# Sixteen-head attentions: scores as one pass over rounded parts and rests, made a second time with the keys on the partitions

## The reference

```
x = x + tanh(g_xattn[0]) * L0_xattn(layernorm(x), ctx, mask, ...)     # stage 0: 16 heads of 8 features, key mask
x = x + tanh(g_ffn[0])   * L0_ffn(layernorm(x), ...)                  # stage 1: 16 experts, 4 taken, and a shared one
x = x + tanh(g_xattn[1]) * L1_xattn(...)                              # stage 2: one head, gated
x = x + tanh(g_ffn[1])   * L1_ffn(...)                                # stage 3: 8-bit fake-quantised weights, LoRA
x = x + tanh(g_xattn[2]) * L2_xattn(...)                              # stage 4: 8 heads of 64
x = x + tanh(g_ffn[2])   * L2_ffn(...)                                # stage 5: 8 experts, 2 taken, and a shared one
x = x + tanh(g_xattn[3]) * L3_xattn(layernorm(x), ctx, ctx, ...)      # stage 6: 16 heads of 8 features, no mask
x = x + tanh(g_ffn[3])   * L3_ffn(layernorm(x), ...)                  # stage 7: 64 experts, 6 taken, and a shared one
```

```
q = heads(x_n @ Wq + bq); k = heads(ctx @ Wk + bk); v = heads(ctx @ Wv + bv)
s = (q . k) / sqrt(8); s = -inf where the key is masked (stage 0)
out = (softmax(s) . v, heads side by side) @ Wo + bo
```

## Time and profile before

| | |
|---|---|
| median of 3 runs | 595.21 us |
| lowest and highest | 591.88 and 597.31 us |
| span of the profiled execution | 594.0 us, 10687 instructions |
| PE, DVE, ACT, POOL busy | 566.0, 381.8, 384.2, 243.2 us |
| the stage-0 attention, from its first scores to the last update of x | 28.1 to 91.1 us |
| the stage-6 attention, the same | 375.6 to 437.6 us |

### The profile page before, as it was taken

How to read it: one execution, slowest core, us unless ns; L and a number is a source line. 1 busy time by engine, 2 the same in 40 slices (tenths; PEclk the granted TensorE clock), 3 DMA queues, 4 the chain that set the end, 5 groups by cost and what they waited for, 6 DMA issues and landing times.

```text
span 594.0 us, 10687 instructions
## 1 busy us (share of the span) xinstructions
PE 566.0 (95%) x3685; PEld 410.5 (69%) x3689; DVE 381.8 (64%) x736; ACT 384.2 (65%) x781; POOL 243.2 (41%) x229
## 2 busy tenths in 40 slices
PE   8999998999999997999799999999999999999997
PEld 6567766787664775777555556577668788888885
DVE  1678865756741647777454666478838666666665
ACT  4277776755666447888675656677875566666663
POOL 5006673485014100111015681000024788888884
PEclk8999998999989999999989999999999999999999
DMA  8300001161000000000000102000001666666650
GB/s 253 144 2 2 2 1 33 20 168 47 7 2 1 0 1 1 1 2 1 2 0 1 40 14 67 1 2 1 2 5 42 163 171 174 184 173 180 183 132 35
DMA packets 14850, 33.54 MB, mean 56 GB/s; under 512 B 2912, under 2 KB 8432, under 8 KB 14672
## 3 DMA queue, kind: packets, MB, share of 16 engines
q1 hardware_dynamic: 14800, 32.89, 19.5%
HBM read 32.03 MB, written 0.85 MB: 55 GB/s over the span
## 4 chain that ended last, share of the span: by engine, by line
PE 76%; DVE 8%; ACT 7%; issue 6%; POOL 2%; DMA 1%; ACTq 0%; DVEq 0%; SPq 0%; POOLq 0%
PE bank L845 9%; PE bank L847 9%; PE bank L846 9%; PE bank L728 5%; PE bank L739 5%; PE bank L754 3%; PE bank L687 3%; ACT wa L1418 2%; PE bank L702 2%; PE bank L650 2%; PE bank L644 2%; PE bank L1253 2%; PE bank L1128 2%; PE bank L1142 2%; PE bank L1117 1%
## 5 line engine op out<-in xcount | busy, mean ns | idle before, releaser
L504 POOL TENSOR_TENSOR h_lo<-wc,h_hi 128x512 fp32r<-128x512 f32 x54 | 70.0, 1300 | 13.7 <-ACT h_hi L1487 13.7
L845 PE MATMUL bank<-xn_hi,w_hi 128*128 128x512 f32 x168 | 66.0, 393 | 3.4 <-DVE xn_lo L1975 3.1
L847 PE MATMUL bank<-xn_hi,w_lo 128*128 128x512 f32 x168 | 65.4, 390 | 0.0
L846 PE MATMUL bank<-xn_lo,w_hi 128*128 128x512 f32 x168 | 65.4, 389 | 0.0
L1964 DVE TENSOR_TENSOR wb<-arena,bank 128x512 f32<-128x512 f32 x64 | 44.0, 687 | 33.0 <-PE bank L847 33.0
L1487 ACT ACTIVATE h_hi<-wc 128x512 fp32r<-128x512 f32 x54 | 34.0, 633 | 37.6 <-DVE wc L1972 27.9
L496 POOL TENSOR_TENSOR w_lo<-ring,w_hi 128x384 fp32r<-128x384 f32 x42 | 42.7, 1019 | 19.1 <-ACT w_hi L1464 19.1
L1746 DVE TENSOR_TENSOR wa<-bank,row_max 128x512 f32<-128x512 f32 x64 | 44.3, 691 | 7.5 <-ACT wb L1364 4.3
L1364 ACT ACTIVATE wb<-wa 128x512 f32<-128x512 f32 x64 | 40.1, 630 | 13.7 <-DVE wa L1746 13.3
L1742 DVE TENSOR_REDUCE row_max<-bank 128x4 f32<-128x512 f32 x64 | 43.6, 682 | 5.9 <-PE bank L728 5.4
L1370 ACT ACTIVATE wc<-bank 128x512 f32<-128x512 f32 x64 | 38.0, 593 | 8.4 <-PE bank L739 7.8
(11 more groups left out here) (351 smaller groups left out, 1392.2 us busy)
## 6 DMA issues: line engine op xcount, KB each, us to landing
arena<-comb_rows SPq DMA_DIRECT2D x64, 256.0 KB, 4.1
ring<-in_experts SPq DMA_DIRECT2D x42, 192.0 KB, 2.5
ring<-in_experts SPq DMA_DIRECT2D x8, 256.0 KB, 4.0
mats<-in_mats SPq DMA_DIRECT2D x1, 1472.0 KB, 10.5
mats<-in_mats SPq DMA_DIRECT2D x1, 832.0 KB, 6.7
mats<-in_mats SPq DMA_DIRECT2D x2, 320.0 KB, 8.2
x<-in_x_t SPq DMA_DIRECT2D x1, 512.0 KB, 4.7
context<-in_ctx_t SPq DMA_DIRECT2D x1, 512.0 KB, 5.0
```

Source lines behind the costliest of these rows:

```text
L504: nc.gpsimd.tensor_tensor(h_lo[:, v % 3, :], hidden_of(v), h_hi[:, v % 3, :].bitcast(f32), ALU.subtract).then_inc(m_h_lo, 1)
L845: mm(out, w, x_, start=start, stop=False)
L846: mm(out, w, x_rest, start=False, stop=False)
L847: return mm(out, w_rest, x_, start=False, stop=stop)
```

## The change

Each group of 32 partitions now carries a head three times (24 partitions), then a mask row (24) and four rows for maxima (25 to 28). After the eviction DVE rounds one of the three copies away: keys become rounded part, rest, rounded part; queries rounded part, rounded part, rest. The product of such rows is the sum of three products, and the operands are of the rounded type f32r, which the other split products of this kernel use. So a head's scores are one f32r matmul of 32 x 128 by 32 x 128.

They are made twice. The first time queries are on the partitions, only for the maxima: DVE takes the largest over keys of two banks (1024 columns) at once, PE turns the 16 columns of maxima (`turn_tops`), and DVE adds them into the maxima rows of `q_rows`, whose partners in `k_rows` are -1 (`take_tops`). The second time keys are on the partitions (`turned_scores`) and the maxima are already subtracted; ACT takes the exponential straight from two PSUM banks, and `probs_v` uses it as it is. The subtraction, the transposes and the copies out of them are gone.

In stage 0 the mask goes into the key rows by a further matmul, ACT evicts all key rows, and the clearing and the largest-weight steps go beside the batches (`beside0`). In stage 6 `k_rows_split(1, n)` stands in stage 5: 0 and 1 ahead of norm 5, 2 and 3 behind it, 4 to 7 between `pick` and `shared(0)`; the query pieces of the first half stand ahead of the attention, those of the second in batches 0 and 1. The diff, cut to its core:

```diff
@@ gpsimd: spread_columns, now 4 copies for a matrix
-                    nc.gpsimd.tensor_copy(dst[:, :, g, :, 0:HD], wide[:, :, g, :, :]).then_inc(w_spread, 1)
+                    for e in range(2):
+                        thrice = dst[:, :, g, e, 0:3 * HD].rearrange("p m (c d) -> p m c d", c=3)
+                        nc.gpsimd.tensor_copy(thrice, wide[:, :, g, e, :].unsqueeze(2).to_broadcast([P, 4, 3, HD]))\
+                            .then_inc(w_spread, 1)
@@ tensor: k_rows_of
+                if inst == 0:
+                    ins = mm(to[:, :], mask_at[:, :], mask_neg[:, c * HALF:c * HALF + HALF], start=False, stop=True)
@@ tensor: attn
+                def by_pair(out_bank, left, right, b, p):
+                    for m_ in range(QUADS):
+                        for r in (2 * p, 2 * p + 1):
+                            rows = slice(32 * r, 32 * r + 32)
+                            last = mm(bank[out_bank + r % 2][:, m_ * P:m_ * P + P],
+                                      left[rows, m_, b * P:b * P + P], right[rows, m_, b * P:b * P + P],
+                                      start=True, stop=True)
+                    return last
                 def scores(b, p):
+                    if tb + b + p > 0:
+                        pe.wait_ge(a_max, 2 * (tb + b) + p)
+                    by_pair(0, q_rows, k_rows, b, p).then_inc(a_s, 1)
+                def turn_tops(b):
+                    pe.wait_ge(a_max, 2 * (tb + b) + 2)
+                    if b > 0:
+                        pe.wait_ge(a_exp, 2 * (tb + b) - 1)
+                    nc.tensor.transpose(bank[2][:, 0:P], top_wide[:, :], ident[:, :]).then_inc(a_top, 1)
+                def turned_scores(b, p):
+                    pe.wait_ge(a_taken, tb + b + 1)
...
+                    by_pair(2 + 2 * p, k_rows, q_rows, b, p).then_inc(a_st, 1)
...
                 scores(0, 0)
+                q_rows_of(inst, 1, range(0, 2))
                 scores(0, 1)
+                q_rows_of(inst, 1, range(2, 4))
                 for b in range(B):
+                    turn_tops(b)
+                    if b + 1 < B:
+                        scores(b + 1, 0)
+                    if b >= 2:
+                        turn_back(b - 2)
+                    if b >= 1:
+                        probs_v(b - 1, 1)
+                    if b >= 2:
+                        through_o(b - 2)
+                    turned_scores(b, 0)
+                    if b + 1 < B:
+                        scores(b + 1, 1)
+                    turned_scores(b, 1)
+                    if b >= 1:
+                        turn_o(b - 1)
+                    probs_v(b, 0)
@@ scalar: attn
+                    fn(probs[p][:, :, :], banks[:, 2 + 2 * p:4 + 2 * p, :], ACT.Exp, scale=SCALE_A).then_inc(a_exp, 1)
@@ vector
+            def rows_split(dst, raw, rounded, rests, done):
+                link(v.tensor_scalar(rounded.bitcast(f32r), raw, rest_cols[:, rests - 1:rests], None, ALU.mult))
+                v.tensor_tensor(dst, raw, rounded, ALU.subtract).then_inc(done, 1)
...
+                largest(0, 0)
+                largest(0, 1)
+                for b in range(B):
+                    take_tops(b)
+                    if b + 1 < B:
+                        largest(b + 1, 0)
+                        if b < 2:
+                            q_rows_split(inst, 4 + 2 * b)
+                        largest(b + 1, 1)
+                        if b < 2:
+                            q_rows_split(inst, 5 + 2 * b)
+                    beside(b)
+                    if b >= 1:
                         divide(b - 1)
@@ vector: stage 0
+            k_rows_split(0, 0)
             norm_rest(0)
+            for n in range(1, 4):
+                k_rows_split(0, n)
...
+            for n in range(4):
+                q_rows_split(0, n)
             for n in range(4, 8):
+                k_rows_split(0, n)
+            def beside0(b):
+                if b in (0, 1):
+                    v.tensor_reduce(w_max[:, b:b + 1], ffn_weights(b), X, ALU.max, apply_absolute_value=True)\
+                        .then_inc(d_rowmax, 1)
+                if b == 2:
+                    dve.wait_ge(d_max, 1)
+                    link(v.tensor_scalar(w_scale, w_max[:, 2:4], 1.0 / 127.0, None, ALU.mult))
+                    link(v.reciprocal(w_inv, w_scale))
+                    v.tensor_scalar(w_neg, w_scale, -1.0, None, ALU.mult).then_inc(d_scaled, 1)
+                if b == 3:
+                    v.memset(comb_pieces[:, :, :], 0.0)
+            attn(0, beside0)
@@ vector: stage 5
+            for n in range(2):
+                k_rows_split(1, n)
             norm(NORM_OF[5][0])
+            for n in range(2, 4):
+                k_rows_split(1, n)
...
             pick()
+            for n in range(4, 8):
+                k_rows_split(1, n)
@@ vector: stage 6
             norm(NORM_OF[6][0])
-            attn(1)
+            for n in range(4):
+                q_rows_split(1, n)
+            attn(1, lambda b: None)
```

More of the change, by code:

```diff
@@ L721, in scores, with probs_v @@
                         pe.wait_ge(a_q_rows, 8 * inst + 8)
-                    if b > 0:
[L723 to L747, removed]
+                    if tb + b + p > 0:
[3 more added lines that the diff above has]
+                    pe.wait_ge(a_max, 2 * (tb + b) + 2)
+                    if b > 0:
+                        pe.wait_ge(a_exp, 2 * (tb + b) - 1)
+                    nc.tensor.transpose(bank[2][:, 0:P], top_wide[:, :], ident[:, :]).then_inc(a_top, 1)
+                def turned_scores(b, p):
+                    pe.wait_ge(a_taken, tb + b + 1)
+                    if b == 0:
+                        pe.wait_ge(a_q_raw, 8 * inst + 8)
+                    else:
+                        pe.wait_ge(a_exp, 2 * (tb + b) + p - 1)
+                    by_pair(2 + 2 * p, k_rows, q_rows, b, p).then_inc(a_st, 1)
+                def probs_v(b, p):
+                    pe.wait_ge(a_exp, 2 * (tb + b) + p + 1)
+                    if p == 0:
                         if b == 0:
@@ L751, in probs_v @@
                             pe.wait_ge(a_ocopy, tb + b)
[L752 to L756, removed]
-                    last.then_inc(a_pv, 1)
[L759 to L768, removed]
-                        nc.tensor.transpose(bank[7][:, 2 * P:3 * P], o_tok[:, :], ident[:, :]).then_inc(a_back, 1)
-                    if u == 3:
-                        pe.wait_ge(a_ofm, yb + b + 1)
-                        mm(bank[7][:, 3 * P:4 * P], w[:, 3 * P:4 * P], o_fm[:, 0, :], start=True, stop=True)\
-                            .then_inc(a_y, 1)
@@ L797, in attn @@
                 else:
-                    keep_warm(2, bank[3])
-                tail(B - 1, 1)
+                    keep_warm(4, bank[3])
+                turn_o(B - 1)
                 if inst == 0:
@@ L1401, in units @@
-                exp(0, 0)
-                over_batches(act, batch)
+                    act.wait_ge(a_y, tb + b + 1)
+                    update(s, y, before + b if before + b > 0 else None, P)
+                for b in range(B):
+                    if b >= 2:
+                        copy_back(b - 2)
+                    if b >= 1:
+                        copy_o(b - 1)
+                    if b >= 2:
+                        batch_update(b - 2)
+                    exp(b, 0)
+                    exp(b, 1)
@@ L1546, in _ @@
             norm_rest(0)
-            for c in range(2):
-                act.wait_ge(a_mask_rows, c + 1)
-                fn(mask_rows[:, c, :], bank[5 + c][:, :], ACT.Copy).then_inc(a_mask_out, 1)
+            act.wait_ge(a_bias_rows, 1)
+            k_rows_out(0, 0, bank[4])
             act.wait_ge(in_mask, 32)
```

269 lines of the change are left out of this document (130 added, 139 removed).

## The result

The changed kernel takes **614.18 us** (median of 5 runs, 611.57 to 623.05) for 595.21: 1.0325 times as long, 95% interval 1.0277 to 1.0373. The forecast was 596, between 587 and 610, so the time lies outside, on the slower side. The changed kernel was run a second time beside its experiments (`again`: 616.53 us, 1.0421 [1.0356, 1.0486]); its trace, span 613.9 us, is nearest the median and is the one read here. The ratios leave out executions far above the fastest of the same kernel; since these kernels can run a loop at either clock, I give the range of the runs too where it is wide.

A forecast was written before the change was run, and what follows sets the result against it. PE's instructions were taken to bound the attention batches. Stage 0 -2.8, stage 5 +7.9, stage 6 -6.5 and clock +2.5 summed to +1.1 us, giving 596 us against 595.21; range 587 to 610.

The forecast's parts named there:

- the clock: Before each attention and in stage 5, PE waits may halve the clock, up to 1.7 us each; 2.5 us in all.
- A one-pass block: In both attentions, a block of eight one-record f32r head scores takes 0.55 us on PE, where plain ones took 1.09.
- The 0.68 by the rule on weight loads: Alternative score block time if load and stream of one row group add up; stage 6 ends about 3 us later.
- The batch: One batch of the new attention loop takes 5.1 us, where it took 6.7.
- the ring of maxima: In each batch, maxima, turn, `take_tops` and next scores wait on each other through shared banks: 4.75 us.
- Rival 1: Narrow one-pass products are not cheap: score blocks of 0.86 to 1.09 us, 609 us in all; chance 24%.
- Split pieces: A scaling and a subtraction of 128 x 512 on DVE take 1.27 us a piece with their link.
- First scores: Query pieces delay the attention's first scores: stage 6 by 2.6 us to 378.2, stage 0 by 2.9 to 31.0.
- Stage 0: First attention gains 2.8 us and no more, because POOL ends it at 88.3 us.
- POOL's start: In stage 0, POOL's steps wait for the scales, ready after batch 2's DVE steps, at about 54.4 us.
- The 33.4 us for POOL's steps: POOL's stretch in stage 0: 30.91 us busy, 33.4 with the gaps between steps.
- Stage 5: Split pieces delay `softmax_route` by 2.8 us and `shared(0)` by 5.1: +7.9 us, bounds 0 and 9.5.

The follow-up runs named there:

- final: Changed kernel plus idle PE products in both attentions, stage-0 largest-weight steps in batch 0, six stage-5 split pieces between `weighed` and `late` in the expert loop: 580.11 us.
- start_fill: Changed kernel with eight idle 128 x 128 x 128 products in each of batches 0 and 1 alone: 603.34 us.
- plain_both: Changed kernel with both score passes as plain float32, twice the score work for PE: 600.98 us.
- the plain loop: Attention loop of the changed kernel with both score passes as plain float32, as in plain_both (600.98 us) and plain_gap (593.45 to 657.58 us).
- plain_gap: plain_both with the step placements of final and one DVE clearing in batch 3 of stage 6: 593.45, 626.64, 657.34 and 657.58 us.
- best_start: start_fill with both stage-0 largest-weight steps in batch 0 and six stage-5 split pieces in expert-loop steps 2 to 12: 603.98 us.
- one_gap: final with one DVE clearing of 128 x 2048 behind the maxima of batch 3 of stage 6: 589.64 us.

## Why the prediction was wrong, point by point

**The step that failed is the clock.** It said: "If it falls, each costs up to 1.7 us; I take half, 2.5 in all; ends 0 and 5." The 3.4 us of a fall were read in a kernel whose work brought the clock back at once; I carried them over to another loop. And "little on PE" misread that row: its fall came at 297.7, with PE busy for most of the time ahead, in part on products of a single column (294.77 to 296.57). In the changed kernel a fall lasted to the end of the attention, 58 us in stage 0 and, but for one stretch of 3.4 us at 1.00, 55 in stage 6. Its price in stage 6: 78.93 against 62.80 us in `final`, or 65.73 in `start_fill`; in stage 0: 96.16 against 83.87 in `final`, or 87.74 in `plain_both`, where the largest-weight steps stand as in the changed kernel. That is 22 to 28 us where the sum had 2.5. The end of the range should have been "at 1.2 GHz all through the attention", and rows 2 and 3 would have given its size: a loop bound by PE at half the clock. By the Trainium skill, "TensorE: Matmul & The Clock Gate", Part 1, the throttled state is the default and sustained matmul activity releases it; by that a loop that keeps PE busy should be at full clock. The trace disagrees for this loop: 43.00 of 43.00 us busy at 0.51. A PE that the profile shows as busy can be at either clock; the granted clock has to be read beside it.

What holds the clock up was shown only by loops. Once down, the one-pass loop and the plain loop stay down; the loop with sixteen transposes a batch doesn't fall at a wait of 1.36 us; one-pass loops with four, six and eight idle 128 x 128 products a batch fall at the start and come back. All of this fits the transposes, which the change was made to remove, as what kept the clock up. More narrow products alone don't do it, since the plain loop has twice those of the loop before and stayed at 0.50 (`plain_gap`). But no run put transposes into the new loop, or took them alone out of the old one, so that they are the cause remains argued.

**A one-pass block**, 0.55: measured 0.50 to 0.54 at full clock, one record a head. Right. The 0.68 by the rule on weight loads of the Trainium skill ("TensorE: Matmul & The Clock Gate", section on row and column packing) did not come out; whether the rule or the 0.11 us put in for a load is at fault isn't shown. **The batch**, 5.1: at full clock 4.45. Too high, since the ring of maxima with its 4.75 does not bind: DVE still waits 0.76 us for PE in such a batch; PE's own sum was 4.7. **Rival 1** forecast 609 with blocks of 0.86 to 1.09; the blocks did take 1.04 and the time was near, but that is a coincidence: it came from the clock, not from what such a product costs, and at full clock the rival was wrong.

**Split pieces**, 1.27: two starts of a piece lie 1.12 us apart where POOL is idle (316.50 and 317.62). Right enough. **First scores** of stage 6, +2.6: norm 6 to first scores grew from 11.25 to 13.31 us, +2.1. Those of stage 0, forecast at 31.0, started at 29.32. **Stage 0**: the mechanism, POOL as the end of the stage at full clock, was right (89.54 in `plain_both` for 88.3), and POOL's start was near, but for another reason than I gave; with the maximum over the partitions a batch earlier (`final`) the last update starts at 84.69. POOL's late first update also held PE up once (0.77 us in `start_fill`), where I had called it covered by slack. The 33.4 us for POOL's steps is about 1 too much: without its waits for ACT the stretch of the earlier trace rows is 32.3, and `plain_both` took 32.8. With the clock as it was, POOL hardly mattered.

**Stage 5**, +7.9: measured +8.7, with PE's wait of 4.38 us where 5.1 was forecast and a clock stretch behind it. Right, and `final` gives it back, 73.98 us for 72.43.

## What to carry to other kernels

When a change takes full-width products off a loop that PE bounds, price the loop at half clock too, and look for PE gaps of a few tenths of a us at its start: a loop can run at either speed, and one gap may decide which. A fall's length read in one loop says nothing about another. Here a few idle products at the right batches, a better place for six DVE steps in stage 5 and the largest-weight steps a batch earlier turned 1.03 into 0.98 with the same way of making the scores.

## What the hardware showed beyond that

The same program had two speeds: `best_start` from 590.75 to 608.72 us, `plain_gap` from 593.45 to 657.58. `final` isn't free of it: one of its six executions took 590.35 us at a mean granted clock of 0.968, that of `one_gap`. POOL's maximum over the partitions, shown as 0.37 us, kept POOL from its next instruction for 7.4 us (46.36 to 53.77), while DVE, in the kernel before, went on with the outcome 0.41 us after the start of that maximum.
